# Graph attention, 8 batches of 2048 nodes: inverse sums behind the next score pass, an earlier mask, the shift's sign on another engine, and output blocks finished in pairs

## The reference

```python
# layer 0: x is (8, 2048, 256), adj (8, 2048, 2048) int32, W (256, 256), a (512, 1)
h = maximum(layernorm(x), 0)
Wh = einsum('bnf,fo->bno', h, W)
f1, f2 = Wh @ a[:256, 0], Wh @ a[256:, 0]
e = f1[:, :, None] + f2[:, None, :]
e = where(e >= 0, e, 0.2 * e)
attention = softmax(where(adj > 0, e, -9e15), axis=1)
out = x + elu(einsum('bij,bjo->bio', attention, Wh))
```

## Time and profile before

| | us |
|---|---|
| median of 3 runs | 1095.69 (1093.25 to 1096.59) |
| profiled execution | 1092.74 |
| its span, first to last instruction | 1091.0 |
| PE busy | 972.8 (89%) |
| DVE busy | 978.4 (90%) |
| ACT busy | 958.3 (88%) |
| POOL busy | 401.7 (37%) |
| DMA queue 1, share of 16 engines | 62.2% |

### The profile page before, as it was taken

The page is one execution under the profiler, slowest core; times in us unless marked ns, Lnnn a source line. Parts: engine busy times, 40 slices in busy tenths (PEclk is TensorE's granted clock), DMA queues, the critical chain, the costliest instruction groups (busy, mean ns, idle before and its releaser), DMA issues. The chain is left out here.

```text
span 1091.0 us, 24411 instructions
## 1 busy us (share of the span) xinstructions
PE 972.8 (89%) x8963; PEld 831.9 (76%) x8963; DVE 978.4 (90%) x1579; ACT 958.3 (88%) x1606; POOL 401.7 (37%) x317
## 2 busy tenths in 40 slices
PE   4667799899999999899998999999999999888987
PEld 3445688788878888787887888787887878777776
DVE  4379999999999999999999999999999999999973
ACT  3368999999999999998999999998999989988974
POOL 2313323334343433334343343334333343333334
PEclk9769999999999999999999999999999999999999
DMA  4366665666676676666766666766766566766614
GB/s 129 113 184 168 167 174 163 193 181 193 190 207 181 180 217 180 189 179 197 200 190 197 180 195 188 208 176 186 211 191 186 172 192 171 198 179 184 180 35 150
DMA packets 325654, 195.11 MB, mean 179 GB/s; under 512 B 9760, under 2 KB 321312, under 8 KB 325536
## 3 DMA queue, kind: packets, MB, share of 16 engines
q1 hardware_dynamic: 325536, 193.56, 62.2%
HBM read 176.69 MB, written 16.84 MB: 177 GB/s over the span
## 5 line engine op out<-in xcount | busy, mean ns | idle before, releaser
L689 POOL TENSOR_TENSOR direct<-prob,inv 128x1024 f16<-128x1024 f32 x128 | 242.6, 1895 | 590.7 <-DVE inv L605 585.2
L589 DVE CUSTOM_DVE_ANT_0 prob<-tp,f_row 128x2048 f32<-128x2048 bf16 x128 | 293.3, 2291 | 4.9 <-issue 4.4
L378 PE MATMUL acc<-v,direct 128*128 128x256 f16 x1024 | 280.2, 274 | 11.1 <-DVE direct L613 6.0
L360 PE MATMUL acc_st<-v,stored 128*128 128x256 f16 x992 | 270.2, 272 | 22.2 <-DVE z_st L629 21.6
L380 PE MATMUL acc<-v,direct 128*128 128x256 f16 x1024 | 279.9, 273 | 0.0
L382 PE MATMUL acc<-v,direct 128*128 128x256 f16 x1024 | 279.9, 273 | 0.0
L362 PE MATMUL acc_st<-v,stored 128*128 128x256 f16 x992 | 270.3, 272 | 0.0
L361 PE MATMUL acc_st<-v,stored 128*128 128x256 f16 x992 | 270.3, 272 | 0.0
L439 ACT ACTIVATE prob<-prob,shift 128x2048 f32<-128x2048 f32 x128 | 256.6, 2005 | 10.8 <-issue 0.4
L432 ACT ACTIVATE prob<-prob,f 128x2048 f32<-128x2048 f32 x128 | 255.6, 1997 | 0.0
L331 PEld LDWEIGHTS tp<-ident_b,neg 128*128 128x128 bf16 x2048 | 119.5, 98 | 94.1 <-issue 92.1
(11 more groups left out here) (71 smaller groups left out, 1222.4 us busy)
## 6 DMA issues: line engine op xcount, KB each, us to landing
raw<-in_adj SPq DMA_DIRECT2D x128, 1024.0 KB, 6.0
x_in<-in_x SPq DMA_DIRECT2D x128, 128.0 KB, 5.0
y<-in_x SPq DMA_DIRECT2D x128, 128.0 KB, 4.6
out<-y SPq DMA_DIRECT2D x128, 128.0 KB, 3.7
f_row<-f_scratch SPq DMA_DIRECT2D x32, 256.0 KB, 5.0
f_scratch<-f_t SPq DMA_DIRECT2D x128, 0.5 KB
w_cat<-in_W SPq DMA_DIRECT2D x1, 256.0 KB, 2.9
prob<-in_a SPq DMA_DIRECT2D x1, 256.0 KB, 3.7
```

The lines of the kernel that those rows point to most:

```text
L360: nc.tensor.matmul(bank[:, 0:FO], p_st[:, 0, rows], v_c[:, 0, :], start=(c == 0), stop=False)
L378: nc.tensor.matmul(acc[:, m, :], p_d[:, 0, rows], v_c[:, 0, :], start=(j == 0 and m % 2 == 0), stop=False, skip_group_check=True)
L589: nc.vector.tensor_tensor_reduce(out=prob[:, c % 2, :], in0=tp_b, in1=f1_row[:, b % 2, :], scale=1.0, scalar=-3.0e38, op0=ALU.add, op1=ALU ...
L689: nc.gpsimd.tensor_tensor(direct[:, c % 2, 0, :], p[:, 0:HALF], k.to_broadcast([P, HALF]), ALU.mult).then_inc(hi_direct, 1)
```

## The change

- DVE: recip_s and inv_total are renamed total_s and small_total. The reciprocal and the scaling of chunk s leave the end of step s and stand in step s+1 right behind mask_scores(s+1), as invert(s).
- DVE: make_mask(s+2) stands ahead of split_low(s-1).
- ACT no longer multiplies by -1; POOL does, in make_shift(s), behind split_high(s-1) and finish_add, ahead of root. ACT's exponential waits for it. The rest of ACT's order stays.
- Blocks are finished in pairs: relu, exponential, elu and add work on 512 elements a partition, the residual load and the output move two blocks in one DMA, and ORDER is a table of pairs.
- Buffers: 6 for 7 of x_in (x is loaded one step later), 4 pairs for 8 blocks of y, 4 for 3 of z_st, 2 pairs for 4 blocks of elu. h_t has one buffer in place of two; the odd chunks below 17 use a stretch of prob that is free until the second score pass.

```diff
@@ -38,11 +38,11 @@
...
     RF = 20
-    RX = 7
+    RX = 6
     RS = 8
-    RY = 8
-    RZ = 3
-    RE = 4
+    RY = 4
+    RZ = 4
+    RE = 2
     R = 4
@@ -67,11 +67,11 @@
...
         z_st = sb("z_st", [P, RZ, FO], F32)
-        elu = sb("elu", [P, RE, FO], F32)
+        elu = sb("elu", [P, RE, 2 * FO], F32)
         x_in = sb("x_in", [P, RX, F], F32)
-        y = sb("y", [P, RY, FO], F32)
+        y = sb("y", [P, RY, 2, FO], F32)
         xn = sb("xn", [P, 2, F], F32)
-        h_t = sb("h_t", [P, 2, KC, P], F32)
+        h_t = sb("h_t", [P, KC, P], F32)
         f12 = sb("f12", [P, 64 + RF], F32)
@@ -81,6 +81,7 @@
...
         ones = prob[0:1, 0, 1024:1024 + P]
+        h_t_early = prob[:, 1, 1024:1024 + F].rearrange("p (k c) -> p k c", k=KC)
         w_nat = w_cat[:, :, 0:FO]
@@ -94,7 +95,7 @@
...
         total = sb("total", [P, R], F32)
-        inv_total = sb("inv_total", [P, R], F32)
+        small_total = sb("small_total", [P, R], F32)
         inv = sb("inv", [P, R], F32)
@@ -132,7 +133,7 @@
...
         prob_ready = sem("prob_ready")
-        recip_s = sem("recip_s")
+        total_s = sem("total_s")
         inv_ready = sem("inv_ready")
@@ -171,6 +172,9 @@
...
 
+        def h_buf(c):
+            return h_t_early if c < LEAD and c % 2 else h_t[:]
+
         FIRST = -24
@@ -210,9 +214,8 @@
...
 
-        ORDER = {2: [0, 8], 3: [1], 4: [2], 5: [3, 9], 6: [4], 7: [5], 8: [6], 9: [7],
-                 10: [10], 11: [11], 12: [12], 13: [13], 14: [14], 15: [15]}
-        ORDER_LAST = {2 + q: [q, 8 + q] for q in range(8)}
+        ORDER = {2: [4], 3: [0], 5: [1], 7: [2], 9: [3], 11: [5], 13: [6], 15: [7]}
+        ORDER_LAST = {2: [4], 3: [0], 4: [5], 5: [1], 6: [6], 7: [2], 8: [7], 9: [3]}
         finish_at = {}
@@ -225,14 +228,15 @@
...
 
-        def output_rows(k):
+        def rows_of(tensor, k):
             b, i = finishing[k]
-            r = (NB + i if i < NB else i - NB) * P
-            return b, slice(r, r + P)
+            r = (NB + 2 * i if i < 4 else 2 * (i - 4)) * P
+            return tensor[b, r:r + 2 * P, :].rearrange("(t p) f -> p t f", p=P)
 
...
             b, i = finishing[k]
-            return z_st[:, i % RZ, :] if i < NB else z_direct[:, i - NB, :]
+            z = z_st[:, 2 * i % RZ:2 * i % RZ + 2, :] if i < 4 else z_direct[:, 2 * (i - 4):2 * (i - 4) + 2, :]
+            return z.rearrange("p t o -> p (t o)")
 
@@ -279,22 +283,20 @@
...
                     load_raw(s + 3)
-                if chunk(s + 25) and s + 25 >= RX:
-                    load_x(s + 25)
+                if chunk(s + 24) and s + 24 >= RX:
+                    load_x(s + 24)
                 if chunk(s + LEAD - 1) and (s + LEAD - 1) % 4 == 3:
...
                     wait(sp, y_out[k % RY], 16 * (k // RY))
-                    bo, rows = output_rows(k)
-                    sp.dma_start(y[:, k % RY, :], x[bo, rows, :]).then_inc(x_res_in[k % RY], 16)
+                    sp.dma_start(y[:, k % RY], rows_of(x, k)).then_inc(x_res_in[k % RY], 16)
                 for k in finish(s - 2):
                     sp.wait_ge(y_ready, k + 1)
-                    bo, rows = output_rows(k)
-                    sp.dma_start(out[bo, rows, :], y[:, k % RY, :]).then_inc(y_out[k % RY], 16)
+                    sp.dma_start(rows_of(out, k), y[:, k % RY]).then_inc(y_out[k % RY], 16)
                 if chunk(s + LEAD) and (s + LEAD) % 4 == 3:
...
             for i in range(RY):
-                sp.wait_ge(y_out[i], 16 * (B * C // RY))
+                sp.wait_ge(y_out[i], 16 * (len(finishing) // RY))
 
@@ -305,7 +307,7 @@
...
                 for k in range(KC):
-                    last = nc.tensor.matmul(wh_bank(c)[:, 0:FW], h_t[:, c % 2, k, :], w_cat[:, k, :],
+                    last = nc.tensor.matmul(wh_bank(c)[:, 0:FW], h_buf(c)[:, k, :], w_cat[:, k, :],
                                             start=(k == 0), stop=(k == KC - 1))
@@ -427,15 +429,13 @@
...
                 f2 = f12[:, f2_col(c):f2_col(c) + 1]
+                wait(act, shift_s, c - R + 1)
                 nc.scalar.activation(most[:, c % R:c % R + 1], top[:, c % R:c % R + 1], ACT.Prelu, bias=f2, alpha=ALPHA
...
                 nc.scalar.activation(p, p, ACT.Prelu, bias=f2, alpha=ALPHA).then_inc(leaky, 1)
-                act.wait_ge(most_s, c + 1)
-                nc.scalar.activation(shift[:, c % R:c % R + 1], most[:, c % R:c % R + 1], ACT.Copy, scale=-1.0
-                                     ).then_inc(shift_s, 1)
                 act.wait_ge(leaky, c + 1)
                 act.wait_ge(shift_s, c + 1)
-                wait(act, recip_s, c - R + 1)
+                wait(act, total_s, c - R + 1)
                 nc.scalar.activation(p, p, ACT.Exp, bias=shift[:, c % R:c % R + 1],
@@ -447,8 +447,8 @@
...
                 act.wait_ge(xt_ready, c + 1)
-                wait(act, wh_ps, c - 1)
-                nc.scalar.activation(h_t[:, c % 2].rearrange("p k c -> p (k c)"), xt_bank(c)[:, 0:F], ACT.Relu
+                wait(act, wh_ps, c - 1 if c < LEAD else c)
+                nc.scalar.activation(h_buf(c).rearrange("p k c -> p (k c)"), xt_bank(c)[:, 0:F], ACT.Relu
                                      ).then_inc(ht_ready, 1)
@@ -464,7 +464,7 @@
...
                 act.wait_ge(direct_done, C * (b + 1))
-                wait(act, elu_ready, C * b)
+                wait(act, elu_ready, G * b)
                 m = slice(4 * h, 4 * h + 4)
@@ -473,8 +473,8 @@
...
                 wait(act, y_ready, k - RE + 1)
-                if i < NB:
-                    act.wait_ge(z_stored, G * b + i + 1)
+                if i < 4:
+                    act.wait_ge(z_stored, G * b + 2 * i + 2)
                 else:
@@ -596,13 +596,11 @@
...
 
-            def reciprocal(c):
+            def invert(c):
                 dve.wait_ge(prob_ready, c + 1)
-                nc.vector.reciprocal(inv_total[:, c % R:c % R + 1], total[:, c % R:c % R + 1]).then_inc(recip_s, 1)
-
-            def scale_inverse(c):
-                dve.wait_ge(recip_s, c + 1)
-                nc.vector.tensor_scalar(inv[:, c % R:c % R + 1], inv_total[:, c % R:c % R + 1], 2.0 ** P_BITS, None,
+                nc.vector.reciprocal(small_total[:, c % R:c % R + 1], total[:, c % R:c % R + 1]).then_inc(total_s, 1)
+                dve.wait_ge(total_s, c + 1)
+                nc.vector.tensor_scalar(inv[:, c % R:c % R + 1], small_total[:, c % R:c % R + 1], 2.0 ** P_BITS, None,
                                         ALU.mult).then_inc(inv_ready, 1)
@@ -624,7 +622,7 @@
...
                 if past >= 0:
-                    k_past = finish_index[(past // G, past % G)]
+                    k_past = finish_index[(past // G, past % G // 2)]
                     dve.wait_ge(elu_ready, k_past + 1)
@@ -637,6 +635,8 @@
...
                     mask_scores(s)
+                if chunk(s - 1):
+                    invert(s - 1)
                 if chunk(s + 23):
@@ -652,6 +652,8 @@
...
                     turn_f1((s + LEAD) // 4)
+                if chunk(s + 2):
+                    make_mask(s + 2)
                 if chunk(s - 1):
@@ -660,13 +662,8 @@
...
                     scale_w()
-                if chunk(s + 2):
-                    make_mask(s + 2)
                 for k in finish(s - 1):
                     finish_elu(k)
-                if chunk(s):
-                    reciprocal(s)
-                    scale_inverse(s)
 
@@ -689,6 +686,12 @@
...
 
+            def make_shift(c):
+                pool.wait_ge(most_s, c + 1)
+                wait(pool, prob_ready, c - R + 1)
+                nc.gpsimd.tensor_scalar(shift[:, c % R:c % R + 1], most[:, c % R:c % R + 1], -1.0, None, ALU.mult
+                                        ).then_inc(shift_s, 1)
+
             def root(g):
@@ -704,14 +707,16 @@
...
                 pool.wait_ge(x_res_in[k % RY], 16 * (k // RY + 1))
-                nc.gpsimd.tensor_tensor(y[:, k % RY, :], y[:, k % RY, :], elu[:, k % RE, :], ALU.add
-                                        ).then_inc(y_ready, 1)
+                pair = y[:, k % RY].rearrange("p t f -> p (t f)")
+                nc.gpsimd.tensor_tensor(pair, pair, elu[:, k % RE, :], ALU.add).then_inc(y_ready, 1)
 
...
                     finish_add(k)
+                if chunk(s):
+                    make_shift(s)
                 if chunk(s + 23) and (s + 23) % 4 == 3:
```

## The result

| | before | changed |
|---|---|---|
| median, us | 1094.89 | 1265.41 (1264.28 to 1266.21) |
| profiled execution's span, us | 1091.0 | 1263.6 |
| ratio of the times | | 1.156 (95% interval 1.154 to 1.159) |

The changed kernel is 15.6% slower. The direction and the main mechanism were as forecast, the size was not: 1232 was said, with 1190 to 1262, and 1265 lies above that range.

The account below looks back on a forecast made before the run. No engine has room to spare, so instruction order decides; the moved inverse stalls DVE on v. Batches, last steps and prologue (+1) add 136.7 us to span 1091.0, giving 1227.7, profiled 1229.4, median 1232; range 1190 to 1262.

Parts of the forecast that it names:

- first batch: No finishing work: 16 steps of 6.89 us, plus 1.1 and the stall's 21.6, make 132.9 for 118.00, +14.9.
- five full batches: Each 146.0 us for 127.04: 119.7 less 0.5, plus 21.6 stall, 4.2 mask held, 1.0 take_direct; five give +95.0.
- chunks 96 to 110: The last chunks with v: 15/16 of a full batch's +19.0, so +17.8.
- last 16 steps: No v, so no stall; L613 waits for POOL's high halves or add; 7.70 us a step, +8 on 115.46.
- the end: Where PE hands out a block every 2.6 us: unchanged.
- the stall: DVE's L595 waits for v, queued on ACT behind L445, which waits for the inverse: idle 1.35 us a step, 21.6 a batch.
- T: End of DVE's inverse in a step; v was forecast at T+1.66, DVE's L595 at about T+1.69.
- The collision of mask and add: POOL's paired add, estimated at 1.12 us, holds DVE's mask: 0.72 or 0.32 us lost, 4.2 a batch.
- The rival without collision: The stall stays but the add doesn't hold the mask: 1200 us; chance 0.18.
- my third rival: v is made before DVE asks for it and the stall vanishes: 1082 us; chance 0.05.
- Sign and pairs: Shift on POOL ready by T+2.7, nothing on the path, up to 10 us at most; pairs save DVE 0.5 a batch.
- Clock: Rival: PE's clock falls as PE pauses longer with the stall, +11, 1243 us; chance 0.08.

Follow-up runs that it names:

- Experiments 1: The changed kernel with only the inverse put back at the end of DVE's step: 1101.75 us, ratio 1.007 to the kernel before.
- experiment 2: The kernel before with only the inverse moved behind the next score pass: 1249.14 us, ratio 1.142.
- experiment 5: The changed kernel with POOL's paired add on 8 of 512 elements: 1226.33 us.
- Experiment 6: The changed kernel with POOL's high halves (L686) on 64 of 1024 elements: 1210.39 us.
- Experiment 3: The changed kernel with ACT's split_high_stored(s-1) moved behind take_f and split_v_high of step s: 1240.13 us, ratio 1.133.
- experiment 4: The changed kernel with the mask back behind the low halves: 1253.59 us.
- experiment 7: The changed kernel with the shift's sign back on ACT and make_shift gone from POOL: 1267.69 us, ratio 1.160 to the kernel before.
- experiment 8: The kernel before with DVE's add_halves moved from behind v's low half to right behind the score pass: 1075.93 us, ratio 0.985.

## Why the prediction was right in kind and 33 us short

Measured against the parts of the sum:

| part | forecast | measured | why |
|---|---|---|---|
| start to first scores | +1 | +0.5 | |
| first batch | +14.9 | +16.5 | a wait of 0.2 a step left out (3.2), less 2.9 in step 0, which has no inverse to wait for (5.45); 1.3 not traced |
| five full batches | +95.0 | +106.8 | 1.6 for that wait and 1.0 too little for the add, 0.6 back from a shorter stall, each batch; 0.4 a batch not traced |
| chunks 96 to 110 | +17.8 | +19.4 | the same |
| last 16 steps | +8 | +24.8 | the mask held by L686 or L686 by the mask, some 15; the wait of 0.2, 1.6 |
| the end | 0 | +4.6 | hold and late exponential |
| together | +136.7 | +172.6 | |

**What bounds it, and the stall: right.** The stall is T+1.65 for T+1.69, 1.29 us of it idle; the forecast wait on L595 of some 150 us is 160.2, of which 152.8 fall after the first 17 chunks of v. ACT was not the bound, PE's order fitted. Experiments 1 and 2 show from both sides that the place of the inverse decides. One reading of the trace before was loose: of the 7.3 us of waits a batch only 5.1 were idle time ahead of L595.

**The collision of mask and add: right, a little too small.** I took 4.2 us a batch with an add of 1.12; the add lasts 1.27, the masks lose 0.95 and 0.55 in the two kinds of step, and taking the add away gives 5.2 (experiment 5). The masks beside the add last 2.16 and 1.77 for 1.22. The rule of the Trainium skill ("SBUF — State Buffer", "Who interferes with whom") by which a vector instruction in a two-port mode and a GpSimd instruction fully block each other agrees with the trace for the mask as well. The rival without collision is out.

**The last 16 steps: wrong, and this is the step that failed.** I wrote there that L613 waits for POOL's L686 until T+2.03, and let the mask's 1.14 run inside that wait at no cost. But the mask stands beside L686, and by the very rule that I used against the add the two can't run together. In 8 steps the mask is held until L686's end, in 7 L686 is held until the mask's; L611 then starts at T+2.95 to T+2.99 instead of T+2.03, 0.9 to 1.0 a step and some 15 us in all, of the 16.8 that are missing. The one step with no mask (chunk 126) has L611 at T+2.02, as I had it. The other 1.6 are the wait of 0.2 below. Experiment 6 bears it out: with L686 cut short the 16 steps take 116.1. The same omission hid a second thing: a stall that covers POOL's pass is worth something, and my third rival, everything gained once v is early (1082), priced only the stall. Experiment 3 came out at 1240, 158 us above it.

**A wait of 0.2 us between the low halves and the score pass: not seen.** mask_scores waits until the low half two chunks back has been written, which is now the instruction just ahead of it, where the mask and the inverse used to stand between:

```profile
603.68 1.27 DVE L616 SCALAR_TENSOR_TENSOR stored<-prob,inv,stored 128x1024 f16<-128x1024 f32 x1
605.08 2.29 DVE L589 CUSTOM_DVE_ANT_0 prob<-tp,f_row 128x2048 f32<-128x2048 bf16 x1
```

The spacing is 1.40 instead of 1.20 in nearly every step without an elu: 1.6 us a batch. It is gone in experiment 4, where the mask stands between again. That its cause is this semaphore is read from the code and the rows; it was not tried by itself.

**The end: priced at nothing, 4.6.** The last inverse waits for an exponential that waits for its own shift. Of it 1.6 go with the sign back on ACT (experiment 7), 4.0 with the add or L686 narrow (41.8 from the last score pass to the end in experiments 5 and 6).

**Sign and pairs.** The sign is off the path, as said. The pairs save DVE no more than forecast (0.60 spacing for twice 0.33). **Clock:** 0.91 in the first batch for 0.93; no lasting fall, the rival is out.

With the hold in the last steps (+15), the wait (+14), the longer add (+6) and the short step 0 (-3) the same sum gives about 1264; the end (+4.6) and the shorter stall (-4) nearly cancel, and some 3 us stay untraced. The hold in the last steps could be had from the order, and the rule that I had already used; the sizes of the wait and of the add could not be read from the trace before.

## What to carry to other kernels

When an instruction that frees another engine is moved later, look at what stands behind the waiter in that engine's queue, not only at the waiter: here nobody needed the inverse early, but v stood behind the one who asked for it. And an overlap rule, once used for one pair of instructions, has to be run over all pairs that the new order puts side by side; an idle engine's work (POOL at 38%) is not free when its instructions hold those of the engine that bounds the kernel. A stall may be hiding such a collision, so its price is not what comes back when it is removed.

## What the hardware showed that I had not expected

- The hold works in both directions: L686 2.82 for 1.89 where the mask started first, mask 2.70 for 1.22 where L686 did. And it passes along: mask 2.70, then add 2.25 for 1.27, low half 2.28 for 1.27, a one-element shift 1.18 for 0.21, in one chain on two engines.
- A small operation is held too: one of DVE's on four elements (L566) took 0.54 instead of 0.17 while POOL's pass ran.
- Statistics, the score pass and v's low half, which read one tensor from SBUF or one from SBUF and one from PSUM, ran beside POOL's L686 at full pace (score pass 2.29 beside it in the kernel before, L595 0.48 in experiment 3, statistics 0.43 in the changed kernel). The mask too reads one tensor from SBUF and is held, so the number of its inputs alone doesn't decide; what sets it apart in the rows is its pace, 2048 elements in 1.22 where the score pass takes 2.29 for as many.
- The first score pass began at 61.7 to 66.9 us in kernels whose instructions up to there are those of the kernel before or nearly (61.9 before, 61.7 in experiment 8, 65.0 in experiment 2); the cause stays open. Differences of a few us between two profiled executions can therefore lie there.
